# A written order of steps for a transformer block on one core: a new order, and low halves that follow their high halves at once

## The reference

```python
h = layernorm(x, g1, b1);  x = attention(h, h,   wq1, wk1, wv1, wo1, bo1) + x
h = layernorm(x, g2, b2);  x = attention(h, ctx, wq2, wk2, wv2, wo2, bo2) + x
h = layernorm(x, g3, b3);  a, gate = split(h @ w_ff1 + b_ff1)
out = a * gelu(gate) @ w_ff2 + b_ff2 + x
```

## Time and profile before

| | us |
|---|---|
| median of 3 runs (2983.34 to 2984.4) | 2983.95 |
| the profiled execution, its own time | 2983.34 |
| its span, first to last instruction | 2981.5 |
| PE busy | 2822.4 (95%) |
| DVE busy | 2468.1 (83%) |
| ACT busy | 2244.1 (75%) |
| POOL busy | 1084.1 (36%) |

### The profile page before, as it was taken

The page is one execution under the profiler, slowest core; times in us unless marked ns, Lnnn a source line. Parts: engine busy times, 40 slices in busy tenths (PEclk is TensorE's granted clock), DMA queues, the critical chain, the costliest instruction groups (busy, mean ns, idle before and its releaser), DMA issues.

```text
span 2981.5 us, 84420 instructions
## 1 busy us (share of the span) xinstructions
PE 2822.4 (95%) x28943; PEld 2210.6 (74%) x28943; DVE 2468.1 (83%) x5160; ACT 2244.1 (75%) x6573; POOL 1084.1 (36%) x2358
## 2 busy tenths in 40 slices
PE   0899999999999999999999999999999999999999
PEld 0677777777777777777787877777777777777777
DVE  7887888878788787988878888787888878888787
ACT  2686968868687785977868688685977869778686
POOL 4242433424244242433424334242432424335242
PEclk9999999999999999999999999999999999999999
DMA  6000000000000000000000000000000000000000
GB/s 210 11 2 16 6 5 16 2 18 4 9 12 2 18 4 9 12 2 20 2 18 4 5 16 2 18 4 10 12 2 18 4 10 12 2 19 2 10 2 9
DMA packets 32245, 41.73 MB, mean 14 GB/s; under 512 B 6140, under 2 KB 29848, under 8 KB 31384
## 3 DMA queue, kind: packets, MB, share of 16 engines
q1 hardware_dynamic: 31768, 35.61, 3.8%
HBM read 27.21 MB, written 8.39 MB: 12 GB/s over the span
## 4 chain that ended last, share of the span: by engine, by line
PE 85%; DVE 6%; ACT 3%; issue 3%; DMA 1%; SPq 1%; DVEq 0%; ACTq 0%
PE group_ps L908 18%; PE group_ps L945 12%; PE group_ps L972 11%; PE group_ps L984 11%; PE score_ps L930 10%; PE group_ps L962 9%; PE group_ps L913 8%; PE score_ps L995 5%; PE group_ps L878 2%; ACT arena L510 1%; DVE arena L711 1%; DVE arena L736 1%; ACT arena L500 1%; DVE arena L768 1%; DVE peak L753 1%
## 5 line engine op out<-in xcount | busy, mean ns | idle before, releaser
L444 POOL TENSOR_SCALAR arena<-arena,share 128x120 f32<-128x120 f32 (+1 forms) x2048 | 842.9, 431 | 1278.8 <-DVE share L761 1275.7
L510 ACT ACTIVATE arena<-score_ps,shift,sc 128x120 f32<-128x120 f32 (+1 forms) x2048 | 1018.4, 527 | 3.7 <-DVE shift L757 3.2
L736 DVE SCALAR_TENSOR_TENSOR arena<-group_ps,arena 128x512 f16<-128x512 f32 (+3 forms) x1152 | 621.6, 563 | 182.3 <-ACT arena L500 162.7
L768 DVE TENSOR_TENSOR arena<-group_ps,arena 128x512 f16<-128x512 f32 (+1 forms) x768 | 493.8, 682 | 40.9 <-ACT arena L520 35.1
L520 ACT ACTIVATE arena<-group_ps 128x512 f16<-128x512 f32 (+1 forms) x768 | 422.1, 605 | 97.1 <-PE group_ps L945 96.9
L500 ACT ACTIVATE arena<-group_ps 128x512 f16<-128x512 f32 (+2 forms) x640 | 385.9, 611 | 123.9 <-PE group_ps L908 104.9
L753 DVE TENSOR_REDUCE peak<-score_ps 128x4 f32<-128x480 f32 (+1 forms) x512 | 473.4, 925 | 2.8 <-PE score_ps L930 2.8
L510 ACT ACTIVATION_READ_ACCUMULATOR arena<-score_ps,shift,sc 128x1 f32 x2048 | 461.0, 225 | 0.0
L945 PE MATMUL group_ps<-ident,arena 128*128 128x128 f32 (+1 forms) x3072 | 419.3, 279 | 0.0
L908 PE MATMUL group_ps<-arena,wq 128*128 128x256 f16 x3072 | 377.2, 274 | 0.0
L945 PEld LDWEIGHTS group_ps<-ident,arena 128*128 128x128 f32 (+1 forms) x3072 | 330.7, 140 | 57.1 <-issue 29.4
(11 more groups left out here) (94 smaller groups left out, 3070.8 us busy)
## 6 DMA issues: line engine op xcount, KB each, us to landing
xin<-in_x SPq DMA_DIRECT2D x32, 256.0 KB, 2.8
out<-xres SPq DMA_DIRECT2D x32, 256.0 KB, 3.1
cin<-in_ctx SPq DMA_DIRECT2D x32, 90.0 KB, 2.1
arena<-in_ctx SPq DMA_DIRECT2D x1, 2880.0 KB, 11.2
arena<-in_L_xattn_wq SPq DMA_DIRECT2D x2, 1024.0 KB, 17.7
arena<-in_L_xattn_wo SPq DMA_DIRECT2D x2, 1024.0 KB, 15.0
arena<-in_L_xattn_w_ff SPq DMA_DIRECT2D x1, 2048.0 KB, 14.5
arena<-in_L_xattn_wk SPq DMA_DIRECT2D x1, 1024.0 KB, 15.4
```

What stands on the lines that cost most here:

```text
L444: nc.gpsimd.tensor_scalar(rows, rows, share[:, p % 4, 2 * h + t:2 * h + t + 1], 2.0 ** BOUND, ALU.mult, ALU.mult).then_inc(probs_ready, 1)
L510: ins = nc.scalar.activation(probs[:, p % 4, h, t, 0:K], score_ps[:, p % 2, h, t * K:t * K + K], ACT.Exp, scale=score_scale[a], bias=shift ...
L736: nc.vector.scalar_tensor_tensor(dst, src, factor, high, ALU.mult, ALU.subtract).then_inc(group_done, 1)
L768: nc.vector.tensor_tensor(probsT[0:R, unit % 4, 1, :], bank[0:R], probsT[0:R, unit % 4, 0, :], ALU.subtract).then_inc(group_done, 1)
```

## The change

Two things change. First, `h_low_half` and `c_low_half` are no longer steps of their own. Their code is now the end of `h_halves` and `c_halves`, so DVE writes `h32`, waits there for ACT's high half, and makes the low half before it does anything else. The steps `hlow` and `clow` are gone from the table, from `BEFORE` (the two transposes ahead of the loop) and from the checks. Second, the whole table is a new one. Otherwise the steps of a turn are the same (184 steps and 1808 matmuls on PE), and none is added or left out.

```diff
 TABLE = """
-k1.A.0 q1.A.0 ctx.A v1.A.2 k1.A.1 scores.0 max.0 k1.A.2 q1.A.1 exp.0 scores.1 max.1 q1.A.3 k1.B.3 share.0
...
+k1.A.3 ctx.A q1.A.0 k1.A.0 k1.A.1 q1.A.1 k1.A.2
+scores.0 max.0 q1.A.2
...
-BEFORE = [(x, s, 1) for x in ("stats", "rows") for s in range(SLOTS)] + [(x, s, 1) for s in range(SLOTS) for x in ("turn", "hlow")]
+BEFORE = [(x, s, 1) for x in ("stats", "rows", "turn") for s in range(SLOTS)]
...
                 ins.then_inc(group_done, 1)
-
-            def h_low_half(turn, step):
-                _, s, n = step
                 dve.wait_ge(h_high, ln_of(turn, s, n) + 1)
                 nc.vector.tensor_tensor(hT[s][:, 1], h32[:], hT[s][:, 0], ALU.subtract).then_inc(h_ready, 1)
...
                                         ALU.mult).then_inc(group_done, 1)
-
-            def c_low_half(turn, step):
-                _, s = step
                 dve.wait_ge(c_high, turn * SLOTS + CTXS[s] + 1)
```

More of the change, by code:

```diff
@@ L85 @@
-inner.B.2 ff2.B.3 ff2.B.4 gate.B.7 inner.B.3 ff2.B.5 turn1.A hlow1.A turn1.B ff2.B.6 ff2.B.7 finish.B hlow1.B
+k1.A.3 ctx.A q1.A.0 k1.A.0 k1.A.1 q1.A.1 k1.A.2
+scores.0 max.0 q1.A.2
+scores.1 exp.0 max.1 q1.B.1 v1.A.0 share.0 norm.0 v1.A.3 exp.1
+scores.2 max.2 v1.A.2 k1.B.1
+scores.3 share.1 exp.2 max.3 v1.B.0 share.2 norm.1 probs.0 norm.2
+scores.4 exp.3 max.4 share.3 q1.A.3 probs.1 k1.B.2 exp.4
+scores.5 max.5 bias.A share.4 norm.3 norm.4 q1.B.0 mix.0 probs.2 exp.5
+scores.6 max.6 share.5 norm.5 mix.1 k1.B.0 probs.3
@@ new lines @@
+scores.7 exp.6 max.7 v1.A.1 mix.2 share.6 probs.4
+scores.8 max.8 exp.7 mix.3 v1.B.2 probs.5
+scores.9 exp.8 max.9 share.7 norm.6 mix.4 probs.6 q1.B.2 exp.9 norm.7
+scores.10 max.10 share.8 mix.5 share.9 norm.8 probs.7 k1.B.3 exp.10
+scores.11 max.11 share.10 mix.6 mix.7 probs.8 exp.11 norm.9
+scores.12 max.12 share.11 out1.A.0 probs.9 norm.10 exp.12 out1.A.1 stats2.A norm.11 mix.8
+scores.13 share.12 max.13 probs.10 q1.B.3 rows2.A mix.9 probs.11
+scores.14 exp.13 turn2.A share.13 max.14 mix.10 norm.12 k2.A.0 v1.B.1 q2.A.0 exp.14 bias.B
@@ new lines @@
+scores.15 max.15 share.14 v1.B.3 probs.12 mix.11
+scores.16 max.16 exp.15 norm.13 share.15 probs.13 v2.A.1 q2.A.1 norm.14
+scores.17 max.17 exp.16 mix.12 share.16 v2.A.0 probs.14
+scores.18 norm.15 exp.17 max.18 mix.13 norm.16 probs.15 q2.A.2 mix.14 share.17
+scores.19 norm.17 mix.15 max.19 exp.18 k2.A.1 share.18 probs.16 out1.B.1
+scores.20 exp.19 max.20 ctx.B probs.17 exp.20 share.19 out1.B.0 norm.18 stats2.B
+scores.21 max.21 norm.19 probs.18 rows2.B share.20 q2.A.3 mix.16 mix.17 exp.21 turn2.B
@@ new lines @@
+scores.30 max.30 norm.28 mix.26 share.29 probs.27 v2.B.1 exp.30
+scores.31 max.31 norm.29 share.30 norm.30 ff1.A.0 probs.28 exp.31 ff1.A.1 share.31 ff1.A.2 probs.29 ff1.A.3 mix.27
+    mix.28 norm.31 probs.30 probs.31 mix.29 ff1.A.4 mix.30 mix.31 gate.A.0 ff1.A.5 gate.A.1 gate.A.2 gate.A.3 out2.B.0
+    inner.A.0 inner.A.1 out2.B.1 stats3.B ff1.A.6 gate.A.4 ff2.A.0 gate.A.5 ff2.A.1 rows3.B inner.A.2 ff2.A.2 ff2.A.3
+    turn3.B ff1.A.7 ff2.A.4 ff2.A.5 ff1.B.0 ff1.B.1 gate.A.6 stats1.A gate.A.7 gate.B.0 stats1.B rows1.A gate.B.1
+    ff1.B.2 inner.A.3 ff1.B.3 rows1.B ff1.B.4 ff2.A.6 inner.B.0 ff2.A.7 gate.B.2 gate.B.3 gate.B.4 ff2.B.0 turn1.A
+    ff1.B.5 inner.B.1 ff1.B.6 gate.B.5 gate.B.6 ff1.B.7 ff2.B.1 gate.B.7 ff2.B.2 ff2.B.3 inner.B.2 inner.B.3 turn1.B
+    ff2.B.4 ff2.B.5 ff2.B.6 ff2.B.7 finish.A finish.B
```

17 lines of the change are left out of this document (9 added, 8 removed).

## The result

The changed kernel takes 3031.22 us (median of 4 runs, 3029.98 to 3031.58) against 2984.18 for the kernel before on the same chip: ratio 1.0157, 95% interval 1.0143 to 1.0172. Three more executions of it took 3026.5 to 3033.4. It is slower by 47 us. The forecast was 2991 with a range up to 3012, so the direction was right and the time lies outside the range.

The account below looks back on a forecast made before the run. PE, 95% busy, was taken as the bound. Savings at the turn's start and new waits summed to +0.5 us a turn, +8 over 16 turns, giving 2991 us; the 8-in-10 range was 2966 to 3012.

Parts of the forecast that it names:

- the bank at k1.A.1: Start of the turn, fifth step: PE's wait for the first step's PSUM bank goes whole, -1.4 us a turn.
- turn2.B: Transpose behind an output projection: too little PE work over the chain to the normalised rows, a new wait, +1.05 us a turn.
- turn3.A: Transpose that already waits for normalised rows: cover and chain stay as they are, 0, up to +0.3 us a turn.
- probs.11: Probs step in the first attention: its norm on POOL stands behind the root of stats2.A, +0.3 us a turn.
- v2.A.1: Projection step behind two probs in a row: finds its bank 0.2 us late.
- even rows: Table rows 4 to 11, first attention: ACT's 3.87 us a row nearly fills PE's 3.9, +0.35 us a turn.
- row 11 into out1.A.0: Row with two mixes and no projection: out1.A.0 must wait for mix.7's low half, 0.3 to 0.4 us.
- The rest: Small waits at scores.23 to 26, a late bank, a lost wait at ff2.B.4, fewer width changes: headed +0.1 us a turn.
- the price of the loop: End of the loop: PE stands 1.85 us while it branches, taken to stay unchanged.
- Turn3.B: Transpose before the last feed-forward steps of B: cover stays about 4.15 us, 0 to 0.4, taken as 0.
- the rival on POOL beside DVE: Norms on POOL beside the merged halves run half as long again: +0.7 us a turn, 3002 us, chance 0.04.
- The merged halves: DVE stands 0.70 us at each low half while ACT rounds; four banks hide most of it, +0.15 us a turn.

Follow-up runs that it names:

- the one with the later bias: The changed kernel, with POOL's bias add for the third layernorm of B held until the low half of h3.B is made: 3002.19 us, ratio 1.0053.

## Why the prediction was wrong

Right in its steps: the bank at k1.A.1 (-1.40 for -1.4); turn2.B, whose wait came as the chain of turn3.A over the same five steps (1.06 for 1.05); turn3.A unchanged; probs.11 and v2.A.1 where they were said to be, probs.11 mis-sized by 0.2. For the even rows one place was right, row 11 into out1.A.0, at about its size; the larger one, probs.7, was not foreseen, so the term is 0.62 for 0.35. That one waits for POOL's norm, and through it for DVE: I had weighed only ACT's 3.87 us a row against PE's 3.9, and DVE's 3.80 are as tight. ACT's records grew (the exp of 256 keys from 583 to 705 ns in the mean), but four of them still take 2.17 us from start to start, so that is no sign of more work. Two slips of addition change nothing: the bare chain of turn2.B is 0.71 + 2.34 + 0.87 = 3.92, not 3.95, and the parts under "The rest" make +0.04, as the sum has them, not the +0.1 of the heading.

Wrong, by size of the miss:

*"At the loop's end PE stands 1.85 us ... I take that as the price of the loop, which stays."* It didn't stay, and it wasn't the whole price. The stop grew by 0.46 a turn, and behind it the clock fell at 11 of 15 starts, 1.7 us each, 1.26 a turn in the mean. Together 1.7 of the 2.6 us a turn that the forecast lacks. Shown: with 12 of 15 branches gone the changed kernel gets 44 us back, the kernel before 21. The new tail alone has brought the longer stop and the falls into the old order. Nor was the 2.03 of before the branch's alone, since 0.99 of it stays without a branch. And the term "-1.4" isn't independent of this one: the wait that it takes out had been the cover for the falls that the old order has.

*Turn3.B: "0 to 0.4, I take 0", and the rival on POOL beside DVE.* I had named the rule of two engines sharing an interface, from the page "GPSIMD Engine Reference" of the Trainium skill, and drawn the wrong side of it: I let POOL's norms get longer, and gave that 0.04. It was DVE that stood, at one place where PE needed it, for a bias add that the new order had put 0.05 us ahead of it, 0.96 a turn. Shown by moving the add: the low half is back at 0.69 and the wait is gone. I had summed durations for that stretch without looking for what POOL does beside it.

*The merged halves, "+0.15".* In the new order the term is near right, since splitting them again gains nothing. But the reason given, that four banks hide a stall of DVE, was not: in the old order the same merge costs 44 us, of which 1.28 a turn is a single wait for a bank behind turn2.A and some 14 us in all are falls behind that wait. What in the new order hides the stalls I haven't isolated; four banks are there in both.

What is open: what, beside the stop, decides on a fall. At the starts of turns every fall but one lies behind a stop of 2.25 us or more, in mid-turn they lie behind a wait of 1.3; there are 11 falls in the changed kernel and 3 in the one with the later bias at equal stops, where the difference is a wait of 0.86 us on PE some 18 us earlier and what it shifts; and turn1.B as the last work before the stop went with more falls in one kernel (7 for 3) and fewer in the other (7 for 11). The falls are counted in one execution of each kernel. I haven't told these apart. Nor was it tried to shorten the stop without moving a step.

## What to carry to other kernels

A stop of the bounding engine at a loop's end isn't a constant: an edit to the last steps changes how much is queued when the last wait is released, and it may carry the clock with it. A wait right behind such a stop may be what hides a fall of the clock; price it as cover before taking it away. Write out several turns per pass before polishing the order; here that gave 21 us, more than any order did. When steps are moved, look what POOL does beside each two-input operation of DVE at its new time, since one of the two will stand for the other's full length.
